# Operands of the first two attention steps built on chip, and the loads of every later step merged into two

## The reference

```python
# attention, 16 heads of 8 channels; y is x after a layer norm without scale or shift
y      = layernorm(x)
scores = einsum('bhtk,bhsk->bhts', heads(y), heads(y)) / sqrt(8)
o      = softmax(scores) @ y                     # (b, h, t, 128)
x      = x + layernorm(concat_heads(o) @ weight) # weight is (16*128, 128)
# a gated feed-forward of three 128x128 matrices on layernorm(x), each row mixed with the row before it
xr, xk = mix(z, z_prev, mu_r), mix(z, z_prev, mu_k)
out    = sigmoid(xr @ W_r.T) * (relu(xk @ W_k.T)**2 @ W_v.T)
x      = x + layernorm(out)
```

## Time and profile before

| | |
|---|---|
| median of 3 runs | 1006.61 us (1005.31 to 1006.96) |
| profiled execution | 1009.22 us; its span from first to last instruction 1007.4 us |
| TensorE busy (matmuls) | 913.3 us, 91% of the span |
| VectorE busy | 867.4 us, 86% |
| ScalarE busy | 750.8 us, 75% |
| GpSimd busy | 327.2 us, 32% |
| first score matmul | at 31.1 us |
| last matmul of `project` | at 967.4 us |

### The profile page before, as it was taken

The page is one execution under the profiler, slowest core; times in us unless marked ns, Lnnn a source line. Parts: engine busy times, 40 slices in busy tenths (PEclk is TensorE's granted clock), DMA queues, the critical chain, the costliest instruction groups (busy, mean ns, idle before and its releaser), DMA issues.

```text
span 1007.4 us, 17595 instructions
## 1 busy us (share of the span) xinstructions
PE 913.3 (91%) x5930; PEld 437.1 (43%) x5930; DVE 867.4 (86%) x1112; ACT 750.8 (75%) x1028; POOL 327.2 (32%) x513
## 2 busy tenths in 40 slices
PE   1699999999999999989999999999999999999932
PEld 1244444444444444444444444444444444444521
DVE  6889998989799998798898899979989988989942
ACT  2577877877877787868878768786887878787731
POOL 1112321451144421633126521345116331255121
PEclk9999999999999999999999999999999999999975
DMA  5699999889898879898888888898988998989700
GB/s 175 148 209 184 205 193 207 194 192 200 175 183 169 177 156 187 190 209 180 171 180 162 177 166 172 176 215 178 189 172 171 198 188 164 181 177 189 142 11 11
DMA packets 100346, 174.42 MB, mean 173 GB/s; under 512 B 21537, under 2 KB 62881, under 8 KB 100257
## 3 DMA queue, kind: packets, MB, share of 16 engines
q0 software_dynamic: 36864, 134.23, 69.0%
q1 hardware_dynamic: 63200, 38.93, 14.0%
q10 hardware_dynamic: 192, 0.13, 0.1%
HBM read 28.51 MB, written 10.49 MB: 39 GB/s over the span
## 4 chain that ended last, share of the span: by engine, by line
PE 54%; POOL 12%; DVE 10%; issue 8%; ACT 8%; DMA 4%; SPq 3%; POOLq 0%; DVEq 0%; ACTq 0%
PE ps_o L443 14%; PE ps_o L445 13%; PE ps_o L444 13%; POOL fnw L291 9%; PE ps_s L426 5%; ACT e_f L537 5%; DVE e_lo L747 4%; DMA e_hi<-e_f 3%; PE ps_r L458 2%; PE ps_r L457 2%; PE ps_r L456 2%; POOL e_hi L326 2%; POOL nw L291 1%; SPq L232 1%; SPq L230 1%
## 5 line engine op out<-in xcount | busy, mean ns | idle before, releaser
L747 DVE TENSOR_TENSOR e_lo<-e_f,e_hi 128x2048 f16<-128x2048 f32 x256 | 584.3, 2282 | 53.3 <-DMA e_hi<-e_f 52.4
L537 ACT ACTIVATE e_f<-ps_s 128x2048 f32<-128x2048 f32 x256 | 481.7, 1881 | 142.2 <-PE ps_s L426 134.7
L443 PE MATMUL ps_o<-e_hi,y_hi 128*128 128x512 f16 x1024 | 391.9, 383 | 11.4 <-DVE o_neg L753 11.2
L445 PE MATMUL ps_o<-e_hi,y_lo 128*128 128x512 f16 x1024 | 389.5, 380 | 0.0
L444 PE MATMUL ps_o<-e_lo,y_hi 128*128 128x512 f16 x1024 | 389.4, 380 | 0.0
L326 POOL DMA_DIRECT2D e_hi<-e_f x256 | 140.5, 549 | 609.2 <-ACT e_f L537 546.6
L549 ACT ACTIVATE part<-ps_r,rden 128x128 f32<-128x128 f32 x512 | 145.4, 372 | 48.3 <-DVE rden L759 48.3
L443 PEld LDWEIGHTS ps_o<-e_hi,y_hi 128*128 128x128 f16 x1024 | 99.9, 98 | 161.2 <-issue 63.4
L445 PEld LDWEIGHTS ps_o<-e_hi,y_lo 128*128 128x128 f16 x1024 | 100.4, 98 | 121.8 <-issue 1.5
L444 PEld LDWEIGHTS ps_o<-e_lo,y_hi 128*128 128x128 f16 x1024 | 100.6, 98 | 92.1 <-issue 2.0
L426 PE MATMUL ps_s<-op_t,op_s 32*128 32x512 f16 x1024 | 102.0, 387 | 25.3 <-ACT e_f L537 16.0
(11 more groups left out here) (133 smaller groups left out, 447.6 us busy)
## 6 DMA issues: line engine op xcount, KB each, us to landing
e_hi<-e_f POOLq DMA_DIRECT2D x256, 512.0 KB, 5.0
op_t<-scr_t SPq DMA_DIRECT2D x508, 32.0 KB, 3.6
op_s<-scr_s SPq DMA_DIRECT2D x512, 16.0 KB, 3.5
scr_s<-yT SPq DMA_DIRECT2D x12, 256.0 KB, 4.9
scr_t<-yT SPq DMA_DIRECT2D x12, 256.0 KB, 4.6
xs<-in_L_attn_x_dram SPq DMA_DIRECT2D x4, 512.0 KB, 7.3
out_dram<-res SPq DMA_DIRECT2D x8, 256.0 KB, 5.3
scr_s<-eighth SPq DMA_DIRECT2D x4, 256.0 KB, 3.2
```

Source lines behind the costliest of these rows:

```text
L443: nc.tensor.matmul(dst, y_hi[:, b % 2, s, :], e_hi[:, ring, g, :], start=(q == 0 and g == 0), stop=False)
L445: mm = nc.tensor.matmul(dst, y_lo[:, b % 2, s, :], e_hi[:, ring, g, :], start=False, stop=(q == 1 and g == 3))
L537: nc.scalar.activation(e_f[:, k % EF_RING], ps_s[:], ACT.Exp, scale=1.0 / ROOT).then_inc(weighed, 1)
L747: dve.tensor_tensor(flat(e_lo[:, ring]), flat(e_f[:, k % EF_RING]), flat(e_hi[:, ring]), ALU.subtract).then_inc(split, 1)
```

## The change

- `first_operands` (VectorE) builds the operands of heads 0 and 1 for the first row in `comb_s` and `comb_t` out of 16 channels of `xs`; TensorE turns them by 16 and 32 transposes of 32 columns into `ps_o` and `ps_r`, ScalarE copies them to `op_s` and `op_t`. The shift of these two steps uses the row's own norm times a constant bound.
- The input of batch 0 comes in two halves; ScalarE normalizes one half. The low part of batch 0 is made on GpSimd.
- `turn_y`, `turn_top`, `spread_top` and `turn_shift` of batch 0 stand behind `score(0)`. SP loads from step 2 on. The first quad's 16-bit copy is made by VectorE (`round_first`) in place of the DMA.
- Output weights: ScalarE sums squares, TensorE adds them over partitions, VectorE takes a power of two from that sum. The means are not removed any more; GpSimd subtracts column 127 from the others, and the sum of others stays as it is. `fsum` goes, and a memset of one column takes its place.
- Shift of every batch: a root from the bits alone with a factor `SLACK`, in place of an inverse root with one refinement. `batch_sqrt` goes.
- `load(j)` issues two DMAs of 128 partitions in place of eight of 32.
- The feed-forward weights are turned at k = 12. The constants of batches 1 to 3 go to scratch at k = 8, 10 and 12.

```diff
-        def op_s_load(j, g):
+        def op_s_load(j):
             rows = slice(j % H * HS, (j % H + 1) * HS)
-            return (op_s[32 * g:32 * g + 32, j % OP_RING, :],
-                    scr_s[batch_of(j)][rows, :, 2 * g * P:(2 * g + 2) * P].rearrange("k i t -> (k i) t"))
+            return (op_s[:, j % OP_RING, :],
+                    scr_s[batch_of(j)][rows].rearrange("k i (g t) -> g (k i) t", g=4))
...
-                for g in range(4):
-                    sp.dma_start(*op_s_load(j, g)).then_inc(op_in[slot], 16)
-                    if j > 0:
-                        sp.dma_start(*op_t_load(j, g)).then_inc(op_in[slot], 16)
+                    sp.wait_ge(scr_const, 16 * B)
+                sp.dma_start(*op_s_load(j)).then_inc(op_in[slot], 16)
+                sp.dma_start(*op_t_load(j)).then_inc(op_in[slot], 16)
...
-            for j in range(OP_RING):
+            for j in range(FIRST, OP_RING):
                 load(j)
...   GpSimd, ahead of its loop
+            pool.wait_ge(w_squared, 1)
+            nc.gpsimd.tensor_tensor(w_raw[:, :, 0:C - 1], w_raw[:, :, 0:C - 1],
+                                    w_raw[:, :, C - 1:C].to_broadcast([P, H, C - 1]), ALU.subtract).then_inc(w_based, 1)
+            low_batch(0)
             mark_batch(0)
...   TensorE
+            def weight_sum():
+                pe.wait_ge(w_squared, 1)
+                nc.tensor.matmul(ps_x[:, 0:1], ones[:], w_sum[:, 0:1], start=True, stop=True).then_inc(w_total, 1)
+            def first_operands():
+                pe.wait_ge(comb_s_ok, 1)
+                pe.wait_ge(comb_const, 1)
+                for h in range(FIRST):
+                    for g in range(4):
+                        for q in range(2):
+                            at = h * 2 * P + q * P
+                            mm = nc.tensor.transpose(f16(ps_o[32 * g:32 * g + 32, 0, :])[:, at:at + P],
+                                                     comb_s[:, 2 * g + q, h].rearrange("p i k -> p (i k)"), ident16[:])
+                mm.then_inc(first_s, 1)
+                pe.wait_ge(comb_t_ok, 1)
+                for h in range(FIRST):
+                    for i in range(RB):
+                        for g in range(4):
+                            here = slice(32 * g, 32 * g + 32)
+                            dst = f16(ps_o[here, 1, :] if h == 0 else ps_r[here, :])
+                            mm = nc.tensor.transpose(dst[:, i * P:(i + 1) * P],
+                                                     comb_t[:, i, h].rearrange("p i k -> p (i k)"), ident16[:])
+                    mm.then_inc(first_t, 1)
...
-                pe.wait_ge(w_centred, 1)
+                pe.wait_ge(w_based, 1)
+                if i == 0: pe.wait_ge(yT_ready, 2)
+                if i == 1: pe.wait_ge(first_t_in, 2)
+                if i == 2: pe.wait_ge(shift_ready, 1)
+                if i == 3: pe.wait_ge(w_split, 1)
...
+            weight_sum()
+            first_operands()
             for k in range(LAST):
+                if k in (LAG, LAG + 1): products(k - LAG)
                 if k < QUADS: score(k)
+                if k == 0: turn_y(0, 0); turn_y(0, 1); turn_top(0); spread_top(0); turn_shift(0)
+                if k == 1: weights_less(0); weights_less(1)
+                if k == 2: weights_less(2)
+                if k == 3: weights_less(3)
+                if 2 <= k - LAG < QUADS: products(k - LAG)
+                if k == 12: turn_ffn_weights()
...   ScalarE
+            square_weights(); keep_weight_sum(); normalize_half(); take_first_s(); take_first_t(0); square_batch(0)
             for k in range(LAST):
                 if k < QUADS: weigh(k)
+                if k == 0: take_y(0, 0); take_y(0, 1); take_first_t(1)
+                if k == 1: take_shift(0)
+                if k == 12: turn_in_ffn_weights()
...
-                if k < 4:
-                    weights_high(k)
+                if k == 3:
+                    for i in range(4): weights_high(i)
...   VectorE
+            def near_root(y, v):
+                step(dve.tensor_scalar(y.bitcast(I32), v.bitcast(I32), 1, None, ALU.logical_shift_right))
+                step(dve.tensor_scalar(y.bitcast(I32), y.bitcast(I32), float(ROOT_BITS), None, ALU.add))
             def batch_bound(b):
...
-                step(dve.tensor_scalar(v, v, 1e-30, None, ALU.max))
-                step(dve.tensor_scalar(a.bitcast(I32), v.bitcast(I32), 1, None, ALU.logical_shift_right))
-                step(dve.tensor_scalar(y.bitcast(I32), a.bitcast(I32), -1.0, float(MAGIC), ALU.mult, ALU.add))
+                near_root(y, v)
-            def batch_sqrt(b):
...
-                step(dve.scalar_tensor_tensor(out=a, in0=y, scalar=-1.0, in1=v, op0=ALU.mult, op1=ALU.mult))
...
-                    dve.tensor_reduce(fsum[:], a[:, :, 0:C - 1], AX.X, ALU.add).then_inc(r_summed, 1)
-                    dve.wait_ge(r_summed, r + 1)
-                    dve.tensor_scalar(a[:, :, C - 1:C], fsum[:].unsqueeze(2), -1.0, None, ALU.mult).then_inc(r_full, 1)
+                    dve.memset(a[:, :, C - 1:C], 0.0).then_inc(r_full, 1)
...
-            batch_sqrt(0)
             batch_shift(0)
-            weight_scale()
             for k in range(LAST):
...
-                if k < 4:
-                    weights_low(k)
+                if k == 2: weight_scale(); weights_low(0); weights_low(1)
+                if k == 3: weights_low(2); weights_low(3)
```

More of the change, by code:

```diff
@@ L206, in _, with keep_eighth @@
             sp.wait_ge(const_ok, 1)
-            for b in range(B):
+            sp.wait_ge(w_in, 16)
+            def keep_eighth(b):
                 sp.dma_start(scr_s[b][:, 3, :], eighth[:]).then_inc(scr_const, 16)
+            keep_eighth(0)
             def keep_hi(b):
@@ L416, in weights_less, with turn_ffn_weights @@
                                  stop=True).then_inc(w_less, 1)
+            def turn_ffn_weights():
+                pe.wait_ge(f_in, 80)
+                pe.wait_ge(w_split, 4)
+                for i in range(3):
+                    mm = nc.tensor.transpose(ps_x[:, i * P:(i + 1) * P], wf[:, i, :], ident[:])
+                mm.then_inc(f_turned, 1)
             def score(k):
@@ L484, in row_part @@
                     mm.then_inc(kv_ps, 1)
[L486 to L490, removed]
-            turn_y(0, 1)
-            turn_top(0)
-            spread_top(0)
-            turn_shift(0)
+            weight_sum()
+            first_operands()
             for k in range(LAST):
+                if k in (LAG, LAG + 1):
+                    products(k - LAG)
                 if k < QUADS:
@@ L526, in take_y @@
                 ge(act, scr_in[b - 1], 7 * 16) if b else None
-                nc.scalar.activation(yT[:, part_, :], f16(ps_x[:]), ACT.Copy).then_inc(yT_ready, 1)
+                src = f16(ps_o[:, 0, :] if b == 0 and part_ == 0 else ps_x[:])
+                nc.scalar.activation(yT[:, part_, :], src, ACT.Copy).then_inc(yT_ready, 1)
             def take_shift(b):
@@ new lines, in keep_weight_sum, with normalize_half @@
+            def keep_weight_sum():
+                act.wait_ge(w_total, 1)
+                nc.scalar.activation(w_sum[:, 1:2], ps_x[:, 0:1], ACT.Copy).then_inc(w_summed, 1)
+            def normalize_half():
+                act.wait_ge(centred, 1)
+                for k in range(HALF):
+                    ins = nc.scalar.activation(yn[:, k, :], xs[:, k, :], ACT.Identity, scale=nw[:, 1, k:k + 1],
+                                               bias=nw[:, 3, k:k + 1])
+                ins.then_inc(act_normed, 1)
@@ new lines, in take_first_s, with take_first_t @@
+            def take_first_s():
+                act.wait_ge(first_s, 1)
+                nc.scalar.activation(op_s[:, 0:FIRST, :].rearrange("p j t -> p (j t)"), f16(ps_o[:, 0, :])[:, 0:FIRST * 2 * P],
+                                     ACT.Copy).then_inc(first_s_in, 1)
+            def take_first_t(j):
+                act.wait_ge(first_t, j + 1)
+                src = f16(ps_o[:, 1, :] if j == 0 else ps_r[:])[:, 0:BANK]
+                nc.scalar.activation(op_t[:, j, :], src, ACT.Copy).then_inc(first_t_in, 1)
@@ L611, in _ @@
                     scale(j)
-                if k < 4:
-                    weights_high(k)
+                if k == 3:
+                    for i in range(4):
+                        weights_high(i)
                 for r, o in rows_at(k):
@@ L692, in batch_bound @@
-                step(dve.tensor_scalar(y.bitcast(I32), a.bitcast(I32), -1.0, float(MAGIC), ALU.mult, ALU.add))
-            def batch_sqrt(b):
-                v, y, a, c = (nr[:, i, :] for i in range(4))
-                step(dve.scalar_tensor_tensor(out=a, in0=y, scalar=-0.5, in1=y, op0=ALU.mult, op1=ALU.mult))
-                step(dve.tensor_tensor(c, a, v, ALU.mult))
-                step(dve.scalar_tensor_tensor(out=y, in0=c, scalar=1.5, in1=y, op0=ALU.add, op1=ALU.mult))
+                                       top_ps(b)[:, 0:H].unsqueeze(1).to_broadcast([P, NB, H]), ALU.mult))
```

(13 more changed lines are left out.)

225 lines of the change are left out of this document (149 added, 76 removed).

## The result

| | median, us | range, us |
|---|---|---|
| before | 1006.79 (4 runs) | 1005.31 to 1007.87 |
| changed | 1040.65 (4 runs) | 1038.09 to 1042.62 |

The ratio is 1.0326, 95% interval 1.0296 to 1.0355: slower by 34 us, where 7.6 us less was forecast. The profiled execution took 1042.62 us, its span 1040.8.

What follows compares the result with a forecast made beforehand. TensorE was taken as the bound once the stream runs, though not quite later. Opening -2.5, loads -2.1, shift -4.0 and feed-forward weights +1.0 sum to -7.6, giving 999.0 us from the median 1006.61; range 992 to 1005.

Steps and rivals of the forecast that it cites:

- Loads: Operand loads in the stream: eight DMAs a step become two of the same bytes; 0 for traffic, -2.1 for a gap.
- the gap before 77.90: TensorE's 2.12 us wait for a late operand load, laid to SP issuing without pause; it goes, -2.1 us.
- The count of about 12,900 completions fewer: Merged operand loads: 16 completion packets fall away per DMA, about 12,900 of 63,200; taken as 0 us.
- Rival (d): Merged loads come in bursts on all 16 DMA engines and delay casts: 1014 or above 1020 us; chance 0.07.
- Opening: Start of the kernel up to `products(2)`, before at 49.84: gain between 1.2 and 4.4 us, taken as 2.5.
- Rival (c): Opening: the wait at `weights_less(3)` sends TensorE back to 1.2 GHz, opening +4.0, total 1005.5 us; chance 0.09.
- Shift: Batches 1 to 3: five small VectorE operations go, shortening TensorE's gaps for `o_neg` by 1.33 a batch, -4.0 us.
- fsum in the tail: Dropping `fsum` for a memset gains 0 in the tail, where GpSimd takes up the row's variance only at 973.66.
- the feed-forward weights: In the stream at k = 12: three transposes on TensorE and ScalarE's wait for them, +1.0 us, at most +2.
- Rival (b): TensorE's gain is taken by the next wait, cast or exponential: -3.3 us in all, 1003.3 us; chance 0.13.

Runs made afterwards that it cites:

- with eight loads: Changed kernel with each step's operands again loaded by four + four DMAs of 32 partitions from step 2 on: 1001.68 us, ratio 0.993.
- two engines: Changed kernel with four loads a step of 64 partitions each, slowest dimension 2: 1300.54 us in one run.
- the eight loads on four engines: Changed kernel with eight loads of 32 partitions, rows reordered to (i, k) so the slowest dimension is 4: 1065.04 us, ratio 1.0578.
- one operand merged, on 4 engines or on 16: Changed kernel with only op_t merged (ratio 1.0068) or only op_s merged (0.9958), on 4 engines; or op_s in one load on 16 engines (0.9953).
- moving the normalization: Changed kernel with eight loads and ScalarE's normalization of the attention row one quad later (offset 8 for 7): 1000.35 us, ratio 0.9937.

## Why the prediction was wrong, step by step

**The step that failed** is "Loads", in the words "of the same bytes ... I take 0". I counted the DMAs, their bytes and their packets over all 16 engines and never asked on how many engines one DMA runs. The term was 0, and -2.1 for the gap before 77.90. Measured on the kernel before it is +44, and on the changed kernel +40 (ratio 1.0326 less 0.993). What the runs showed in its place: a merged load has 4 completions and not 16, so it runs on 4 engines, and these are then late with the casts (7.3 us for 5.0) and with the loads. The count of about 12,900 completions fewer was wrong by the same error: SP's queue lost 15,680 packets.

**Rival (d)** had the right sign and the wrong mechanism. It priced the burst as if all 16 engines took it, 0.6 us, and asked when the slack of a quad would be used up. Nor did the merged loads bring larger packets: those of 512 B and more are 78,163 with them and 78,169 with eight loads. The better account is not a burst but a rate. Four engines carry 16 packets of casts and 64 rows of loads a step. With the page's shares this is 5.4 + 2.6 = 8.0 us: 65.7% of 1040.8 us by 16 engines over 36,720 packets is 0.30 each, 18 a step with the completions; 11.7% over 47,520 is 0.041 each, 64 a step. The stream took 954 us for 126 steps, 7.6 a step. The estimate is 5% high; for two engines, 5.4 + 5.1 against some 9.6 (about 1209 us of stream in 126 steps), it is 9% high. It gives the order and about the size, no more, and the eight loads on four engines (1.0578) lie outside it.

**Opening, -2.5.** Measured -2.9 in the changed kernel and -3.6 with eight loads (46.28). The size is right because errors cancel in part, and that is luck. `weights_less(3)` starts at 34.50 and not at 38.1: the transposes of 32 columns ran side by side (the 16 behind the first 16 start 0.40 us later, the low bound and not the serial 2.06), and GpSimd's subtraction took 3.6 and not 5.5, though VectorE's `yn` beside it took 3.3 us longer. The wait in front of it came as described, 3.58 us. From there to `products(2)` it took 12.4 us and not 10.5: half a quad of products ran at the lower level, 1.3 us, and `op_t` of step 2 was late by 0.79.

**Rival (c)**, the clock behind that wait, was in part true. TensorE was at the higher level before it (0.39 at 30.53) and at the lower one behind it: `weights_less(3)` takes 2.04 where 1.13 is the higher level's, and the first products take 0.63 each and reach 0.38 at 38.84. Six of them at 0.21 more each are 1.3 us, where the rival had priced two quads at 2.6. The rule on the clock gate of the Trainium skill, "TensorE: Matmul & The Clock Gate", Part 1, which the prediction names, holds in this trace.

**Shift, -4.0.** Measured -5.7 alone, interval -3.6 to -7.9, which takes in the forecast. The mechanism was right; it left most of the first gap of each pair standing, and that went in two batches of three.

**Gap before 77.90, -2.1.** With eight loads again it did not go but moved: 1.58 us before 87.6. SP was not relieved there. In the changed kernel it was, and the gap is larger: 3.22 us before 83.57. With one operand merged, on 4 engines or on 16, TensorE never waits for `op_t` from 60 to 950 us, so a relieved SP does remove it, as forecast; yet none of these kernels is faster than the one with eight loads (0.9953 at best against 0.993). Two loads on 16 engines each weren't run.

**fsum in the tail, 0, and the feed-forward weights, +1.0** weren't tried alone. TensorE's gap in front of the last row's transposes is 17.6 us before and after, so there is no gain there, as forecast.

**Rival (b)**, gaps that come back, fits the rest but is not shown by the times: opening and shift alone sum to about -9, with the +1.0 for the feed-forward weights -8, and all of it with eight loads is -7.1 (interval -3.7 to -10.4). The traces show it in one place: moving the normalization took 10.0 us from TensorE's wait for `e_f` and gave 8.4 to that for `o_neg`.

## What to carry to other kernels

Before merging DMAs, work out the slowest dimension of both access patterns. Here a pattern that begins with a group of 4 put the transfer on 4 engines, even though it writes 128 partitions. Count the completions: change one kind of load, and divide the difference of the packets under 512 B by the number of DMAs. A landing that gets longer while the mean DMA share falls was the sign of it here. A queue whose transfers nobody waits for can still set the time, when it crowds a few engines that another queue's transfers need.

## What had not been expected of the hardware

- Eight loads of 32 rows on 4 engines cost some 25 us more than two loads of 128 rows on 4 engines. SP's issues become slow (none under 0.61 us) and the loads late; why is open.
- One VectorE operation of 0.34 us took 3.6 beside a GpSimd subtraction of 3.6.
- Transposes of 32 columns to four groups of partitions: 16 in 0.63 us at the lower clock, against 8 of 128 columns in 1.03 in the same kernel.
- An idle spell of 2.07 us on TensorE at the same place was followed by the lower clock level in one kernel (0.58 to 0.63 from 46.05) and not in two others (0.39). Its length alone doesn't decide.
